# A wider GpSimd decay and a new order of VectorE's recurrence steps in a gated linear-attention and mixture-of-experts block

## What is computed

```
S = S * exp(gkt)[..., None]
sab = einsum('bhk,bhkv->bhv', at, S)
S = S + kt[..., None] * (sab[..., None, :] + vt[..., None, :])
ot = einsum('bhk,bhkv->bhv', qt, S)
```

## Time and profile before

| What | us |
|---|---|
| median of 3 runs (lowest, highest) | 1285.74 (1285.09, 1288.67) |
| the profiled execution's own time | 1293.3 |
| its span, first to last instruction | 1291.5 |
| VectorE, TensorE, GpSimd, ScalarE busy | 1191.7, 946.7, 746.7, 393.6 |
| first pair of chunk 0, 4, 7, 28 starts | 51.12, 276.18, 418.75, 1083.44 |
| VectorE idle between 299 and 354, in 17 waits | 22.4 |
| results of expert tiles 0 and 1 written from 372.66 to | 393.4 |
| first landing, last landing start | 421.10, 1053.83 |
| GpSimd in chunks 28 to 31: residual sum, spread, output scales | 0.7, 1.3, 1.4 |
| decay of pair 255, start and end | 1262.10, 1262.82 |

### The profile page before, as it was taken

How to read it: one execution, slowest core, us unless ns; L and a number is a source line. 1 busy time by engine, 2 the same in 40 slices (tenths; PEclk the granted TensorE clock), 3 DMA queues, 4 the chain that set the end, 5 groups by cost and what they waited for, 6 DMA issues and landing times.

```text
span 1291.5 us, 17716 instructions
## 1 busy us (share of the span) xinstructions
PE 946.7 (73%) x3773; PEld 686.2 (53%) x3774; DVE 1191.7 (92%) x3673; ACT 393.6 (30%) x1047; POOL 746.7 (58%) x830
## 2 busy tenths in 40 slices
PE   5888887000092899999999999999999912466763
PEld 2343333000072677777888787788777802345542
DVE  3799999998499999999999999999999999888992
ACT  3444444100030223222333232223223203355552
POOL 3765566277600666666666666666666665465663
PEclk9888889555587899999999999999999955677786
DMA  5665654563422555566666655566666334454432
GB/s 165 199 191 168 204 180 147 130 208 118 122 93 79 155 178 178 173 187 187 187 187 187 183 182 180 179 187 187 178 194 191 82 96 95 119 170 125 147 90 66
DMA packets 247253, 202.62 MB, mean 157 GB/s; under 512 B 141425, under 2 KB 225233, under 8 KB 247185
## 3 DMA queue, kind: packets, MB, share of 16 engines
q1 hardware_dynamic: 170146, 82.81, 24.6%
q10 hardware_dynamic: 70224, 100.49, 23.6%
q0 software_dynamic: 6816, 18.69, 4.3%
HBM read 139.42 MB, written 62.54 MB: 156 GB/s over the span
## 4 chain that ended last, share of the span: by engine, by line
DVE 69%; issue 17%; PE 4%; DMA 3%; SPq 2%; ACT 2%; another core or an unknown queue 1%; POOL 1%; DVEq 0%; POOLq 0%; ACTq 0%
DVE obh L1128 10%; DVE psB L1154 7%; DVE outer L1168 7%; DVE state L1187 6%; DVE psB L1176 6%; DVE ubuf L1154 5%; DVE prod_a L1145 4%; DVE prod_q L1181 3%; DVE psB L1164 2%; DVE prod_q L312 2%; PE psA L930 2%; DVE ubuf L1156 2%; DVE work L984 1%; DVE psB L1166 1%
## 5 line engine op out<-in xcount | busy, mean ns | idle before, releaser
L306 POOL TENSOR_TENSOR decayed<-state,rbh 128x256 f32<-128x256 f32 x200 | 145.8, 729 | 310.1 <-DVE state L1187 178.7
L862 PE MATMUL psA<-xgT,wts 128*128 128x256 f32 x1248 | 288.2, 388 | 36.4 <-ACT work L683 35.5
L874 PE MATMUL psF<-wts,work 128*128 128x256 f32 x1248 | 288.7, 384 | 3.5 <-ACT work L683 3.0
L862 PEld LDWEIGHTS psA<-xgT,wts 128*128 128x128 f32 x1248 | 236.5, 193 | 85.5 <-ACT work L683 40.4
L874 PEld LDWEIGHTS psF<-wts,work 128*128 128x128 f32 x1248 | 230.8, 190 | 49.7 <-issue 15.8
L323 POOL TENSOR_TENSOR prod_q<-state,rbh 128x512 f32<-128x512 f32 x175 | 223.4, 1277 | 0.0
L1128 DVE TENSOR_REDUCE obh<-prod_q 128x16 f32<-128x272 f32 x512 | 217.8, 426 | 0.0
L683 ACT ACTIVATE work<-psA,b_sb 128x256 f32<-128x256 f32 x312 | 129.9, 470 | 204.7 <-PE psA L862 149.8
L1145 DVE TENSOR_TENSOR prod_a<-state,psT 128x512 f32<-128x512 f32 x224 | 153.7, 686 | 13.2 <-remote 4.8
L694 ACT ACTIVATE work<-psF,work 128x256 f32<-128x256 f32 x78 | 36.9, 473 | 257.1 <-PE psF L876 257.1
L850 PE MATMUL psT<-ident,work 128*128 128x128 f32 x156 | 24.2, 279 | 105.5 <-DMA work<-xs_d 105.4
(11 more groups left out here) (166 smaller groups left out, 1471.7 us busy)
## 6 DMA issues: line engine op xcount, KB each, us to landing
wts<-in_L_ffn_W_dram ACTq DMA_DIRECT2D x78, 1024.0 KB
rec_d<-work SPq DMA_DIRECT2D x32, 640.0 KB
rbh<-rec_d SPq DMA_DIRECT2D x32, 640.0 KB
xs_d<-zero SPq DMA_DIRECT2D x26, 387.0 KB, 8.3
work<-xs_d ACTq DMA_DIRECT2D x39, 258.0 KB
wts<-y_d ACTq DMA_DIRECT2D x16, 512.0 KB, 5.3
x_acc<-in_L_attn_x_dram SPq DMA_DIRECT2D x32, 128.0 KB
og_d<-work SPq DMA_DIRECT2D x32, 128.0 KB, 7.9
```

The source lines that it names most:

```text
L306: eng.tensor_tensor(decayed[:, :, :], state[:, g % SR, :, :], over_v(rbh[:, u, 2 * n + 1, F_:F_ + HD]), ALU.mult).then_inc(s_dec, 1)
L862: mm = pe.matmul(psA[m // 2 % 2][:, m % 2 * MT:(m % 2 + 1) * MT], w1_sb[v][:, c, m * P:(m + 1) * P], xgT[:, c, :], start=(c == 0), stop=(c ...
L874: pe.matmul(psF[q][:, 0:D], hT[:, m, q * P:(q + 1) * P], w2_sb[v][:, m, :], start=(m == 0), stop=False)
```

## The change

For chunks 7 to 31, GpSimd's decay (`read_and_decay`) becomes one 512-wide instruction: state times a2 and state times decay, into `prod_a[:, n, 1]` and `prod_a[:, n, 2]`. VectorE's L1145 makes only the first step's product there (256 wide), and both row sums, the first outer product and the wait for GpSimd now stand ahead of the second reduction (`two_shared_steps`). Chunks 0 to 6 have a function of their own, with all operands in SBUF, one reduction for both steps, and the last row sum behind the new state. `prepare` writes a2 in place, and copies only a1 to PSUM, from chunk 7 on. The array `decayed` and the constant HOMED go; PAIR_STEP is 3.7. In the hunk of `two_steps` only the new code is shown; the old stands above.

```diff
@@ -44,10 +44,9 @@
...
-HOMED = 4
...
-PAIR_STEP = 3.95
+PAIR_STEP = 3.7
...
@@ -148,8 +147,7 @@
...
-        decayed = sb("decayed", [P, HD, HD])
-        prod_a = sb("prod_a", [P, NP, 2, HD, ROW])
+        prod_a = sb("prod_a", [P, NP, 3, HD, ROW])
...
@@ -162,7 +160,7 @@
...
-        home_a = psT[1][:, 0:RING * HD].rearrange("p (t k) -> p t k", t=RING)
+        home_a = psT[1][:, 0:NP * HD].rearrange("p (n k) -> p n k", n=NP)
...
@@ -293,7 +291,7 @@
...
-            return 8 * (c + 1) + max(0, c + 1 - HOMED)
+            return 8 * (c + 1) + max(0, c + 1 - SHARED)
...
@@ -301,10 +299,13 @@
...
-        def decay(eng, g):
+
+        def read_and_decay(eng, g):
...
-            eng.tensor_tensor(decayed[:, :, :], state[:, g % SR, :, :], over_v(rbh[:, u, 2 * n + 1, F_:F_ + HD]),
-                              ALU.mult).then_inc(s_dec, 1)
+            wide = [P, 2, HD, HD]
+            eng.tensor_tensor(prod_a[:, n, 1:3, :, 0:HD], state[:, g % SR, :, :].unsqueeze(1).broadcast_to(wide),
+                              rbh[:, u, 2 * n + 1, A_:A_ + 2 * HD].rearrange("p (j k) -> p j k", j=2)
+                              .unsqueeze(2).broadcast_to(wide), ALU.mult).then_inc(s_dec, 1)
...
@@ -541,7 +542,7 @@
...
-                decay(pool, g)
+                read_and_decay(pool, g)
...
@@ -1097,21 +1098,19 @@
...
-                home = home_a.rearrange("p (n j) k -> p n j k", j=2)
...
-                dve.tensor_copy(prod_a[:, :, :, :, HD].rearrange("p n j v -> p (n j) v"), rbh[:, u, :, V_:V_ + HD])\
-                    .then_inc(s_prep, 1)
+                dve.tensor_copy(prod_a[:, :, 0:2, :, HD], tok[:, :, :, V_:V_ + HD]).then_inc(s_prep, 1)
...
-                dve.tensor_tensor(home[:, :, 1, :] if c >= HOMED else a2, a2, f1, ALU.mult).then_inc(s_prep, 1)
+                dve.tensor_tensor(a2, a2, f1, ALU.mult).then_inc(s_prep, 1)
...
-                if c >= HOMED:
-                    dve.tensor_copy(home[:, :, 0, :], a1).then_inc(s_prep, 1)
+                if c >= SHARED:
+                    dve.tensor_copy(home_a, a1).then_inc(s_prep, 1)
...
@@ -1127,64 +1126,78 @@
...
+            def two_steps(g, tile=None):
                 n, u, par = g % NP, g // NP % 2, g % 2
                 old, new = state[:, g % SR, :, :], state[:, (g + 1) % SR, :, :]
+                u1, u2 = ubuf[:, par, 0, :], ubuf[:, par, 1, :]
+                decayed = prod_a[:, n, 2, :, 0:HD]
                 done = g * CHAIN + 1
                 if tile is not None and tile < NT:
                     silu(tile)
                 dve.wait_ge(s_chain, done)
+                dve.tensor_tensor(prod_a[:, n, 0:2, :, 0:HD], old.unsqueeze(1).broadcast_to([P, 2, HD, HD]),
+                                  rbh[:, u, 2 * n:2 * n + 2, A_:A_ + HD].unsqueeze(2).broadcast_to([P, 2, HD, HD]),
+                                  ALU.mult).then_inc(s_chain, 1)
+                dve.tensor_tensor(decayed, old, over_v(rbh[:, u, 2 * n + 1, F_:F_ + HD]), ALU.mult).then_inc(s_dec, 1)
+                dve.wait_ge(s_chain, done + 1)
+                dve.tensor_reduce(ubuf[:, par, :, :], prod_a[:, n, 0:2, :, :], AX.X, ALU.add).then_inc(s_chain, 1)
+                if g > 0:
+                    read_left(dve, g)
+                if g > 2:
                     sum_row(g - 2, 0)
+                dve.wait_ge(s_chain, done + 2)
+                dve.scalar_tensor_tensor(out=u2, in0=u1, scalar=pair[:, 0, n:n + 1], in1=u2, op0=ALU.mult, op1=ALU.add)\
+                    .then_inc(s_chain, 1)
+                dve.tensor_tensor(outer[:, 0, :, :], over_v(rbh[:, u, 2 * n, K_:K_ + HD]), over_k(u1), ALU.mult).then_inc(s_chain, 1)
                 dve.wait_ge(s_chain, done + 3)
                 dve.tensor_tensor(outer[:, 1, :, :], over_v(rbh[:, u, 2 * n + 1, K_:K_ + HD]), over_k(u2), ALU.mult)\
                     .then_inc(s_chain, 1)
                 if tile is not None:
                     scale_k(tile - 1)
                     if tile < NT:
                         square_sums(tile)
+                dve.wait_ge(s_chain, done + 4)
                 dve.wait_ge(s_dec, g + 1)
+                dve.tensor_tensor(decayed, decayed, outer[:, 0, :, :], ALU.add).then_inc(s_chain, 1)
+                read_found(dve, g)
                 dve.tensor_scalar(prod_q[:, g % SR, 1, :, HD], u1, pair[:, 1, n:n + 1], None, ALU.mult).then_inc(s_chain, 1)
                 if tile is not None:
                     scale_a(tile - 1)
+                dve.wait_ge(s_chain, done + 6)
+                dve.tensor_tensor(new, decayed, outer[:, 1, :, :], ALU.add).then_inc(s_chain, 2)
+                if g > 1:
+                    sum_row(g - 2, 1)
+
+            def two_shared_steps(g, out_tile=None):
+                n, u, par = g % NP, g // NP % 2, g % 2
+                old, new = state[:, g % SR, :, :], state[:, (g + 1) % SR, :, :]
+                u1, u2, raw = home_u[:, par, 0, :], home_u[:, par, 1, :], ubuf[:, par, 1, :]
+                done = g * CHAIN + 1
+                if out_tile is not None and out_tile < NT - 1:
+                    gate_o(out_tile)
+                dve.wait_ge(s_chain, done)
+                dve.tensor_tensor(prod_a[:, n, 0, :, 0:HD], old, over_v(home_a[:, n, :]), ALU.mult).then_inc(s_chain, 1)
+                sum_row(g - 2, 0)
+                dve.wait_ge(s_chain, done + 1)
+                dve.tensor_reduce(u1, prod_a[:, n, 0, :, :], AX.X, ALU.add).then_inc(s_chain, 1)
+                sum_row(g - 2, 1)
+                dve.wait_ge(s_chain, done + 2)
+                dve.tensor_tensor(home_o, over_v(rbh[:, u, 2 * n, K_:K_ + HD]), over_k(u1), ALU.mult).then_inc(s_chain, 1)
+                dve.wait_ge(s_dec, g + 1)
+                dve.tensor_reduce(raw, prod_a[:, n, 1, :, :], AX.X, ALU.add).then_inc(s_chain, 1)
+                dve.tensor_scalar(prod_q[:, g % SR, 1, :, HD], u1, pair[:, 1, n:n + 1], None, ALU.mult).then_inc(s_chain, 1)
+                dve.wait_ge(s_chain, done + 4)
+                dve.scalar_tensor_tensor(out=u2, in0=u1, scalar=pair[:, 0, n:n + 1], in1=raw, op0=ALU.mult, op1=ALU.add)\
+                    .then_inc(s_chain, 1)
+                dve.wait_ge(s_chain, done + 3)
+                dve.tensor_tensor(home_o, prod_a[:, n, 2, :, 0:HD], home_o, ALU.add).then_inc(s_chain, 1)
+                dve.wait_ge(s_chain, done + 6)
+                dve.tensor_tensor(outer[:, 1, :, :], over_v(rbh[:, u, 2 * n + 1, K_:K_ + HD]), over_k(u2), ALU.mult)\
+                    .then_inc(s_chain, 1)
                 if out_tile is not None and out_tile < NT - 1:
                     out_stats(out_tile)
+                dve.wait_ge(s_chain, done + 8)
+                dve.tensor_tensor(new, home_o, outer[:, 1, :, :], ALU.add).then_inc(s_chain, 1)
                 if out_tile is not None and out_tile >= LAG:
                     gated(out_tile - LAG)
                 for q, (lo, hi) in enumerate(NORMS):
@@ -1193,15 +1206,17 @@
...
-                if c == HOMED:
+                if c == SHARED:
...
-                    two_steps(c * NP + n, slots + n if slots is not None and slots + n <= NT else None,
-                              outs + n if outs is not None else None)
+                    if shared(c * NP + n):
+                        two_shared_steps(c * NP + n, outs + n if outs is not None else None)
+                    else:
+                        two_steps(c * NP + n, slots + n if slots is not None and slots + n <= NT else None)
...
```

More of the change, by code:

```diff
@@ L1128, in sum_row @@
                 dve.tensor_reduce(obh[:, c % OB, row % RING, :], prod_q[:, g % SR, side, :, :], AX.X, ALU.add).then_inc(s_o, 1)
-            def two_steps(g, tile=None, out_tile=None):
+            def two_steps(g, tile=None):
                 n, u, par = g % NP, g // NP % 2, g % 2
-                homed = g // NP >= HOMED
                 old, new = state[:, g % SR, :, :], state[:, (g + 1) % SR, :, :]
-                where = home_u if homed else ubuf
-                u1, u2 = where[:, par, 0, :], where[:, par, 1, :]
-                raw = ubuf[:, par, 1, :]
-                out1 = home_o if homed else outer[:, 0, :, :]
-                coef = home_a[:, 2 * n:2 * n + 2, :] if homed else rbh[:, u, 2 * n:2 * n + 2, A_:A_ + HD]
+                u1, u2 = ubuf[:, par, 0, :], ubuf[:, par, 1, :]
+                decayed = prod_a[:, n, 2, :, 0:HD]
                 done = g * CHAIN + 1
@@ L1141, in two_steps @@
                     silu(tile)
-                if out_tile is not None and out_tile < NT - 1:
-                    gate_o(out_tile)
                 dve.wait_ge(s_chain, done)
-                dve.tensor_tensor(prod_a[:, n, :, :, 0:HD], old.unsqueeze(1).broadcast_to([P, 2, HD, HD]),
-                                  coef.unsqueeze(2).broadcast_to([P, 2, HD, HD]), ALU.mult).then_inc(s_chain, 1)
-                if not shared(g):
-                    decay(dve, g)
-                elif g > 2:
-                    sum_row(g - 2, 0)
@@ L1151, in two_steps @@
-                dve.wait_ge(s_chain, done + 1)
```

(30 more changed lines are left out.)

## The result

The change takes 1253.08 us (median of 4, 1251.86 to 1253.64), the kernel before in the same comparison 1287.2 (median of 4, 1285.09 to 1289.22): ratio 0.9734, interval 0.9713 to 0.9754. The profiled execution after took 1252.75 with a span of 1251.0.

The account below looks back on a forecast made before the run. VectorE's instruction order was taken as the bound. Gains of 5.3 and 21.3, cut to 17.9 at the hand-over, less 3.2, gave 14.7 us: 1293.3 to 1278.6, less 7.6 for the median: 1271.0; own range 1264 to 1279, wider 1256 to 1284.

Parts of the forecast that it names:

- The waits of VectorE between 299 and 354: Chunks 4 and 5: waits of 22.4 us taken as unchanged; bounds: all gone, or half as much again.
- R4: Rival: the scatter stretch changes; 15 us more ends at 1286, waits gone near 1252; chance 0.08, half each.
- R5: Rival: a consumer right behind its producer costs nothing extra; pair 3.42, 18 us less by pair 223: 1253; chance 0.03.
- In the other pairs of chunks 0 to 3: Pairs other than the last of chunk 3: no gain, as a gate product already stood in the gap.
- Chunks 4 to 6: Pair step falls from 4.71 to 4.54 us, 0.17 x 24 = 4.1 us gained.
- Chunks 7 to 27: Pair step 3.53, net gain 0.13 a pair with landings counted, over 167 pairs up to pair 223: 21.3 us.
- the bare dependence: A VectorE consumer directly behind its producer starts 0.44 later instead of 0.33, a cost of 0.11 us.
- The hand-over: At chunk 28: later last landing, behind pair 223, holds pair 225 until 1069.8; the lead falls from 26.7 to 17.9 us.
- R1: Rival: the hand-over is hidden, as y loads and fetches come quicker; 1262; chance 0.15.
- Chunks 28 to 31: Pairs gain 7.8; late decays cost 5.7, the last pair's decay 1.7, locked gate products 3.6: 3.2 us lost.
- R2: Rival: GpSimd becomes the bound from chunk 28, 10 us more: 1281; chance 0.12.
- R3: Rival: the wide decay of chunks 7 to 27 is late in every pair; about 1338; chance 0.04.

Follow-up runs that it names:

- c1: The changed kernel with both row sums between product and reduction in chunks 7 to 31, first outer product right behind its reduction: 1274.58 us, ratio 0.9881 to before.
- e4: The changed kernel with PAIR_STEP 3.85 instead of 3.7, so the last landing is due at pair 219: 1239.69 us, ratio 0.9744 to before.

## Why the prediction was wrong

- **"The waits of VectorE between 299 and 354 ... I leave as they are"** is the step that failed. They went, and with them 22.4 us of the profiled execution's lead and some 12 of the medians' 34. They go with the PSUM form of chunks 4 to 6, which the change takes away (1272 without it beside a before of 1287); how that form makes them is open. I had that edit in view only as 0.17 a pair. The half of R4 in which they go said near 1252 and had 4 in 100, although all of them lay in the only stretch whose operands the change moved from PSUM to SBUF. That its 1252 is nearly the measured 1253 is luck: 1271.0 less 22.4 is 1248.6, the medians hold only some 12 us of waits, and the rest comes from the terms below. R5's 1253 is chance as well; c1 rules it out.
- **"In the other pairs of chunks 0 to 3 ... nothing"** failed too. The pairs step by 6.21 to 6.30 instead of 6.56, and chunk 7 has 9.9 where I had 5.3. My reason, that a gate product stood in the gap already, was right as far as it went; I did not follow the moved row sum back to the instructions that it had stood in front of, and to GpSimd, who waits for one of them.
- **Chunks 4 to 6**, 4.54: measured 4.54 to 4.55. Right.
- **Chunks 7 to 27**, 21.3: measured 21.9 and 22.0. The mechanism is right: the wide decay of 1.27 measured 1.277, the bare dependence 0.11 measured 0.13 by the experiment that adds one. That the sum is so close is partly luck: the pair is 3.56 for 3.53, which loses some 5 us, and a landing costs about 0.08 a tile for 0.22, which gives 5 back.
- **The hand-over**, 26.7 to 17.9, a loss of 8.8: measured 9.0 in the first pair of traces, 8.7 in the second, both at the start of pair 225, as the fetch's chain was right. GpSimd's chain was mis-sized: 16.1 from landing to square sums where I took 13.0 from a trace in which the fetches came 9 us later. The missing 3.1 is VectorE's wait within pair 225, so that by pair 226 the loss is 12.0 in both pairs of traces. R1 is ruled out, and e4's plan, which gains those 12 by moving the landings, confirms the cause.
- **Chunks 28 to 31**, 3.2 lost: from pair 226 on, 2.1 lost in the first pair of traces, 3.6 gained in the second. Before's own end is not steady (181.4, 184.7 and 186.2 from pair 223 to 255 in three profiles, with different waits for TensorE, for fetches and for a decay), so the term can't be judged more closely. Its parts: the late decays took 1.45 (forecast 1.6), the last pair's wait 2.87 for 1.33 (1.54, forecast 1.7), the gate product 1.38 for 0.83 (0.55, as forecast), but nine times instead of six or seven.
- **R2 and R3**: from pair 226 on VectorE waits some 10 us for the decay in the first trace of the change and 7 in the second, where I had 5.7 + 1.7 on top of before's 1.3, and R2 ten more than that. In chunks 7 to 27 there is no wait for it worth the name: R3 is out.
- **The sum.** Without the waits the profiles give 9.9 + 22.0 - 12.0 + 3.6 = 23.5 for my 5.3 + 21.3 - 8.8 - 3.2 = 14.6; the misses are 4.6 ahead of chunk 7, 0.7 in the loop, -3.2 at the hand-over and 6.8 at the end. On top come the waits. The 7.6 that I took off to come from the profiled execution to the median were probably in part these waits: the profile has 22.4 us of them, the medians of two comparisons differ by 13.7. If so, the correction hid that they vary from one execution to the next.
